# Holding GpSimd behind VectorE's second norm, and two steps of VectorE's order moved, in a gated cross-attention and FFN kernel

## What is computed

```python
Sim   = (h @ w1)[:, :, None] + (ctx @ w2)[:, None, :] + einsum('bid,bjd->bij', h * w3, ctx) + b   # h = layernorm(x)
A     = softmax(Sim, axis=2);  hq = A @ ctx
Batt  = softmax(max(Sim, axis=2), axis=1);  hc = Batt @ h          # one row per batch
x1    = x + tanh(g0) * (concat[h, hq, h * hq, h * hc] @ W_qv + b_qv)
y     = layernorm(x1)                                              # the "second norm"
out   = x1 + tanh(g1) * ffn(y)     # ffn: y, three 4-bit block-quantized weights and all intermediates quantized
```

## Time and profile before

| what | value |
|---|---|
| median of 3 runs | 456.11 us (455.79 to 456.21) |
| the profiled execution's own time | 455.91 us |
| its span, first to last instruction | 454.1 us |
| PE busy | 433.1 us (95%) |
| DVE busy | 363.0 us (80%) |
| ACT busy | 275.0 us (61%) |
| POOL busy | 110.9 us (24%) |
| mean granted TensorE clock | 0.992 |

### The profile page before, as it was taken

The page is one execution under the profiler, slowest core; times in us unless marked ns, Lnnn a source line. Parts: engine busy times, 40 slices in busy tenths (PEclk is TensorE's granted clock), DMA queues, the critical chain, the costliest instruction groups (busy, mean ns, idle before and its releaser), DMA issues.

```text
span 454.1 us, 6771 instructions
## 1 busy us (share of the span) xinstructions
PE 433.1 (95%) x2432; PEld 297.5 (66%) x2432; DVE 363.0 (80%) x652; ACT 275.0 (61%) x346; POOL 110.9 (24%) x109
## 2 busy tenths in 40 slices
PE   4899999999999589999999999999999999999997
PEld 3888898889888478644444444444444444788886
DVE  6776769886897869885444799999898889897884
ACT  2677456556524212393434599998297779987760
POOL 1249444465747531100000013344000000000000
PEclk9999999999999979999999999999999999999999
DMA  7950002000200110200000000000000000344442
GB/s 242 318 169 0 1 2 93 1 0 1 94 1 0 40 54 0 94 0 0 0 0 1 0 1 1 0 0 0 1 0 0 0 0 0 118 140 140 139 139 71
DMA packets 20672, 21.13 MB, mean 47 GB/s; under 512 B 825, under 2 KB 20392, under 8 KB 20648
## 3 DMA queue, kind: packets, MB, share of 16 engines
q1 hardware_dynamic: 20628, 20.82, 14.6%
q10 hardware_dynamic: 20, 0.00, 0.0%
HBM read 12.43 MB, written 8.39 MB: 46 GB/s over the span
## 4 chain that ended last, share of the span: by engine, by line
PE 42%; DVE 26%; issue 20%; ACT 6%; POOL 4%; DMA 1%; ACTq 0%; POOLq 0%; DVEq 0%
PE ps L781 12%; PE ps L746 9%; PE ps L751 5%; DVE cols L1454 4%; DVE yb L1182 4%; PE ps L580 3%; PE ps L574 2%; PE ps L576 2%; DVE hid L1470 2%; ACT hid L1010 2%; PE ps L543 2%; PE ps L562 2%; POOL h L418 1%; ACT ag L1015 1%; DVE st L1169 1%
## 5 line engine op out<-in xcount | busy, mean ns | idle before, releaser
L746 PE MATMUL ps<-xh,wuh 128*128 128x512 f16 x192 | 72.8, 379 | 1.2 <-DVE gq L1493 1.1
L746 PE MATMUL ps<-xh,wul 128*128 128x512 f16 x192 | 72.8, 379 | 0.0
L751 PE MATMUL ps<-xl,wuh 128*128 128x512 f16 x192 | 57.1, 379 | 0.0
L1433 DVE TENSOR_REDUCE cols<-hid x10 | 22.9, 2286 | 24.3 <-ACT hid L987 24.3
L781 PE MATMUL ps<-wdh,oh 128*128 128x256 f16 x168 | 37.4, 273 | 0.0
L781 PE MATMUL ps<-wdl,oh 128*128 128x256 f16 x168 | 37.4, 273 | 0.0
L746 PE MATMUL ps<-xh,wgh 128*128 128x512 f16 x96 | 36.4, 379 | 0.0
L746 PE MATMUL ps<-xh,wgl 128*128 128x512 f16 x96 | 36.4, 379 | 0.0
L987 ACT ACTIVATE hid<-ps 128x2048 f32 x10 | 18.7, 1875 | 27.5 <-PE ps L751 27.5
L746 PEld LDWEIGHTS ps<-xh,wuh 128*128 (+1 forms) x192 | 18.8, 98 | 24.4 <-issue 2.1
L480 POOL PARTITION_ALL_REDUCE cols<-cols x4 | 1.5, 365 | 135.3 <-DVE cols L1393 129.2
(11 more groups left out here) (223 smaller groups left out, 1039.3 us busy)
## 6 DMA issues: line engine op xcount, KB each, us to landing
x_scratch<-xa SPq DMA_DIRECT2D x4, 1024.0 KB, 4.6
xo<-x_scratch SPq DMA_DIRECT2D x16, 256.0 KB, 2.7
out_dram<-xo SPq DMA_DIRECT2D x15, 256.0 KB, 2.2
xa<-in_x SPq DMA_DIRECT2D x3, 1024.0 KB, 12.1
xa<-in_x SPq DMA_DIRECT2D x4, 256.0 KB, 4.4
wv<-in_L_xattn_W_qv SPq DMA_DIRECT2D x1, 1024.0 KB, 7.9
wr<-in_L_ffn_w_gate SPq DMA_DIRECT2D x1, 768.0 KB, 10.9
wr<-in_L_ffn_w_up SPq DMA_DIRECT2D x1, 768.0 KB, 12.2
```

The source lines that it names most:

```text
L746: pe.matmul(ps[hf][:, q, :], w_[:, d, ds(k * P, P)], xh[:, d, n], start=d == 0 and w_ is wh, stop=False)
L751: mm = pe.matmul(ps[hf][:, q, :], wh[:, d, ds(k * P, P)], xl[:, d, n], start=False, stop=d == KD - 1)
L1433: dve.tensor_reduce(gmx[:, ds(k * 2 + hf, 1)], unit(hid, k, hf), AX.X, ALU.max, apply_absolute_value=True).then_inc(gm_done, 1)
```

## The change

Three edits of program order; no instruction is added or removed but semaphore waits on POOL.

1. POOL, after each `y_std(n)` (n = 0..14), waits until VectorE's norm of the same pair is done (`y_rdy` at least n+1).
2. VectorE: `summary(3)`, the last batch's matrix, moves within step 18 from behind `residual(11)` to the step's start. `weight_values(2)` moves from near the start of step 18 to its end.
3. VectorE: `weight_unit(2)` moves from the end of step 17 to the end of step 18, ahead of `weight_values(2)`.

```diff
@@ POOL, loop over m
                 if LAG <= m < L + LAG:
                     y_std(m - LAG)
+                    pool.wait_ge(y_rdy, m - LAG + 1)
                 if s == 2 and 1 <= b < B:
                     row_add(b - 1)
@@ VectorE, loop over m
                 late = s == 3 and b < B
+                if m == N + 2:
+                    summary(b - 1)
                 if 4 <= m <= N + 3:
                     attended(m - 4)
                 if m == N:
                     scored(m - 1)
                     batch_max(b - 1)
-                if m == VALUES_AT[2]:
-                    weight_values(2)
@@
                 if LAG <= m and not late:
                     residual(m - LAG)
-                if m == N + 2:
-                    summary(b - 1)
                 if 1 <= m < N:
                     scored(m - 1)
@@
                 for i in range(3):
                     if m == SCALES_AT[i]:
                         weight_scales(i)
-                    if m == W_AT[i]:
+                    if m == W_AT[i] + (i == 2):
                         weight_unit(i)
-                    if m == VALUES_AT[i] and i < 2:
+                    if m == VALUES_AT[i]:
                         weight_values(i)
```

## The result

The changed kernel takes **448.36 us** (448.27 to 448.39, 4 runs) against 455.95 us (454.93 to 456.21, 4 runs) of the kernel before: ratio 0.9837, 95% interval 0.982 to 0.9854. The forecast was 448.5 in a range of 446.3 to 451.6. The profiled span went from 454.1 to 446.4 us.

The account below looks back on a forecast made before the run. VectorE sets the pace between 147.9 and 158.0 us; PE is nearly full before 142.5 and from 190. VectorE's chain gains 7.6 of PE's possible 10.0 us: 456.11 - 7.6 = 448.5 us, range 446.3 to 451.6.

Parts of the forecast that it names:

- The wait on POOL: Pairs 9, 10 and 12: norms shorten by 2.1, 3.6 and 2.4 us; PE's 2.18 us wait for pair 10 goes.
- The matrix first: Step 18: the last batch's matrix is done at 152.6, just when PE needs it; PE's 5.47 us wait goes.
- VectorE's chain: From 152.6 its pieces sum to 14.6 us; the weight's parts end at 167.2, 7.55 us earlier.
- The clock: After PE's 5.47 us wait, loads at granted clock 0.50 take 2.1 us more, part of PE's possible 10.0 us gain.
- The cost at step 15: Third batch's matrix ready at 124.6 to 125.2 instead of 124.29, costing PE 0.3 to 0.9 us, swallowed later; taken as 0.
- gains are worth nothing: Steps before 16: PE is full there, so gains count for nothing and only losses could count.
- PE idle time appears before 142: A sign, before 142 us in the profile, that would show the prediction wrong.
- Rival (b): POOL's hold only changes its victim; two more holds, 2.8 + 1.3, leave 3.5 us of gain: 452.6 us; chance 0.20.
- L1165 (one input in PSUM): This VectorE instruction's staying at 0.74 us was read as agreeing with the rule on which instructions POOL holds.
- Rival (c): Step 18: ACT's copies wait behind the third weight's values, costing once those end after about 161.8; slower, chance 0.05.
- Edit 3: The third weight's later steps cost 3.1 us in VectorE's chain that stand there anyway, now behind pair 11.
- POOL's own times stay what they are: Around pair 10's norm: the norm instruction stands still while POOL's runs, POOL's durations being the same as elsewhere.

Follow-up runs that it names:

- e7: The kernel before with only POOL's second weight_n (L411) one step later; 453.98 us against 455.92 beside it.
- e4: The changed kernel with POOL's wait only from step 16 on (pairs 9 to 14); 447.69 us.
- e1: The kernel before with only POOL's wait for VectorE's norm added; 451.64 us against 455.65 beside it.
- e5: The changed kernel with POOL's L411 also held until the last batch's matrix and the prT behind it are done; 447.47 us.
- e3: The changed kernel with the third weight's unit and values back in their old places; 447.98 us.
- e6: The changed kernel with third weight's unit and values in old places, POOL's wait only from step 16, L411 held until matrix and prT; 445.83 us.
- e2: The changed kernel without POOL's wait, leaving only VectorE's new order; 454.66 us against 455.65 for the kernel before.

## Why the prediction was right

It was right in the time (448.5 for 448.36), in the mechanism, and in most of its terms. That the time fits to 0.14 us is partly luck. The chain gave 7.2 us where the sum had 7.6, and about half a microsecond came from parts of the kernel that the sum left alone.

- **The wait on POOL.** All norms are short, as foreseen. Pair 10's ends at 148.2 where the walk had 147.6 (152.75 before). The late start is pair 9's: its norm starts at 139.89 where the walk had 139.2. From its end to residual(10) it is 4.0 us as foreseen (4.05), with the second weight's values and `prT` behind one POOL instruction each (they take 1.74 and 1.76 us). The 3 us to spare took it up. That it is the missing collision is shown by e7: with L411 moved the second norm instruction falls from 2.86 to 0.40 us, and the one that L411 now meets takes 2.86.
- **The matrix first.** Foreseen: first instruction held to 152.2, both done at 152.6, PE in need of it at 152.6. Measured: 153.17, and PE at 153.50. The matrix is 0.6 us late, because L411, behind the later norm, ends at 152.50 instead of 151.9. PE is 0.9 us late, mostly by the stall at 125. The forecast left no margin here, and the 0.3 us that there are come from PE's lateness: in e4, without that stall, PE waits 0.26 us for the matrix.
- **VectorE's chain.** From the matrix to the end of the first three parts 14.6 us foreseen; measured 14.3 (153.17 to 167.47). Its end was foreseen at 167.2 and measured at 167.47, project(14) at 167.7 and 167.97.
- **The clock.** Of the 10.0 us that PE could gain, 2.1 were put to the slow clock. All four runs of the changed kernel have a mean clock of 1.0; e1's runs, with and without the drop, differ by 1 to 1.7 us. No run takes the drop alone out of the kernel before, so the 2.1 is not measured; e1 speaks for somewhat less. The estimate of 3.4 by the Trainium skill's page "TensorE: Matmul & The Clock Gate" (Terms), throttled time x (1 - K/N), counts the whole 6.8 us; in the first 2.3 of them PE only waited. No difference between runs of one kernel here comes to as much.
- **What was covered.** The cost at step 15 was put at 0.3 to 0.9 us. The matrix is ready at 125.01, within the foreseen 124.6 to 125.2, and PE takes it 0.8 us later than before, measured from L552. PE's wait is 1.49 us because it arrives 0.7 us earlier: "gains are worth nothing", said of the steps before 16, overlooked the waits at 85 us. So the sign "PE idle time appears before 142", named for being wrong, did show, without harm. The cost was taken as 0 at the end; e4, which removes it, gains 0.3 us in the distance.
- **Rival (b)**, the hold that changes its victim, happens, but the two more holds that it needed for 452.6 did not come: the matrix stands behind L411, as in the sum, and the scales' instruction L1282 behind L443. In e1 it is `prT`, in e7 the norm of pair 11. The Trainium skill's rule ("SBUF — State Buffer", Who interferes with whom), that the engine which issues first blocks the other for its whole instruction, fits these rows.
- **A wrong reading.** The prediction takes L1165 (one input in PSUM), at 0.74 us in the earlier trace rows, as a sign that this form isn't held. No POOL instruction ran beside either of the two instances shown. The form is not held all the same: in e5 L1168 takes 0.74 us from 151.75 on, while L411 runs from 151.91.
- **Rival (c)**, ACT's order in step 18, did not come true: the third weight's values end at 160.87 (160.4 foreseen), and PE waits for no copy of ACT there. The foreseen cover of 1.4 us is 1.2 by its own terms, since 157.3 + 1.34 + 5.1 is 163.7 and not 163.9.
- **Edit 3** was taken for neutral in the sum ("stand there anyway"). It isn't: e3 is 1.2 us shorter in the trace without it, and e6 against e5 shows about as much in the times. In e3 the unit stands where VectorE would otherwise wait; the change moved it to where it doesn't. This is a term that the sum had wrong.

One statement was wrong without harm: that POOL's own times stay what they are. VectorE holds POOL as well. POOL, the changed kernel:

```profile
142.14 2.00 POOL L431 TENSOR_TENSOR h<-h 128x512 f32<-128x512 f32 x1
144.21 1.61 POOL L433 TENSOR_TENSOR h<-h 128x512 f32<-128x512 f32 x1
```

L431 takes 1.27 us at 115.85 in the earlier trace rows; here it stands behind the second weight's values (141.26 to 143.00) for its first 0.9 us.

How the gain divides: the wait alone gives 4.0 us, the order alone 1.0 (2 where the clock falls only once), together 7.6 to 7.8. The rest over their sum is what only both do, by these traces: the order alone leaves the wait for y of pair 10, the wait alone that for the matrix, and the mean clock was below 1.00 in all ten runs of the one and three of four of the other. What stays open: the distance accounts for 7.2 us of the 7.7 by which the span is shorter; the other half microsecond lies before step 2 (0.1) and in the FFN part, and no experiment followed it.

## What to carry to other kernels

Where VectorE and GpSimd work side by side, read the durations of one form of instruction, shortest against longest, and lay the long ones beside GpSimd's timeline. Here the held ones ended shortly behind the GpSimd instruction: the norm 0.15 us, the matrix 0.28, `prT` in e1 0.54.

A semaphore wait that makes GpSimd start behind the urgent instruction can then be worth its idle time (4.0 us of gain for 0.85 us of POOL idle at each pair in e1). But the hold lands on the next instruction, so put something there that is not held or not awaited (e5, e6). The wait was needed only in the stretch in which VectorE sets the pace (e4). Leave work that nobody is waiting for where the engine waits anyway; moved behind the urgent work it joins the chain (e3, e6).

## What the runs showed that I had not expected

- The clock did not follow from the length of the wait alone. It dropped in three of four runs of e1, whose trace has a wait of 3.7 us. It was 0.51 soon after a wait of 2.18 us in e2's trace, while after the same 2.18 us in the kernel before it stayed at 1.00 until into the next wait.
- A VectorE TENSOR_SCALAR on two columns was held (L1179, 1.11 us in e5), one on a single column was not: L1281 takes 0.15 us in the changed kernel at 158.58, while L443 runs. Nor was a RECIPROCAL on two columns: L1149 takes 0.17 us in the kernel before at 116.63, while L431 runs.
